# A GPS layer on one core: a histogram in the gather stage replaced by a search in the second norm, which is rewritten, and scalings moved between VectorE and ScalarE

## The reference, cut to what matters

```python
xn = layernorm(x)
x  = x + gcn(xn, src, dst) + linear_attention(xn)
x  = x + gat_experts(layernorm(x), src, dst)
# gcn:  h = relu(batchnorm(xn @ w1.T + b1)) @ w2.T + b2;  xw = h @ w_gcn.T
#       out[d] = sum over edges (s,d) and loops of xw[s] * dinv[s] * dinv[d], + b_gcn
# gat:  h = (x @ W_gat) as 4 heads x 4 experts; e = leaky_relu(a_src[src] + a_dst[dst])
#       softmax of e over the edges of each dst; agg = sum alpha * h[src]
#       layernorm, mean over heads -> scores; top 2 of 4 experts, softmax -> weights
#       out = sum over experts of weight * (gelu(x @ W1 + b1) @ W2 + b2)
```

## Time and profile before

| | before |
|---|---|
| median of 3 runs | 4779.59 us |
| lowest to highest | 4776.38 to 4796.87 us |
| profiled execution, its time | 4790.88 us |
| its span | 4789.0 us |
| PE busy | 3688.3 us, 77% |
| PEld busy | 2442.9 us, 51% |
| DVE busy | 2604.3 us, 54% |
| ACT busy | 880.5 us, 18% |
| POOL busy | 3085.5 us, 64% |

### The profile page before, as it was taken

The page is one execution under the profiler, slowest core; times in us unless marked ns, Lnnn a source line. Parts: engine busy times, 40 slices in busy tenths (PEclk is TensorE's granted clock), DMA queues, the critical chain, the costliest instruction groups (busy, mean ns, idle before and its releaser), DMA issues. The chain is left out here.

```text
span 4789.0 us, 44151 instructions
## 1 busy us (share of the span) xinstructions
PE 3688.3 (77%) x13162; PEld 2442.9 (51%) x13162; DVE 2604.3 (54%) x6218; ACT 880.5 (18%) x1738; POOL 3085.5 (64%) x3019
## 2 busy tenths in 40 slices
PE   3667888888798998787887564799999999700377
PEld 1355555455555555555555354466666666500255
DVE  5946776666666556666666364134334333312476
ACT  2653222222100000000000011222222223200232
POOL 2515777777776776777777500777777777777630
PEclk7989999999887998777677655899999999955689
DMA  6645444444454664333333765444444334322588
GB/s 178 188 98 152 129 130 132 130 130 130 125 154 132 182 177 131 89 91 89 92 91 89 71 193 137 132 114 113 138 115 113 117 106 138 97 63 63 114 209 196
DMA packets 262492, 606.63 MB, mean 127 GB/s; under 512 B 88254, under 2 KB 144369, under 8 KB 256893
## 3 DMA queue, kind: packets, MB, share of 16 engines
q0 software_dynamic: 124496, 304.94, 24.1%
q1 hardware_dynamic: 137772, 299.02, 22.2%
HBM read 447.85 MB, written 155.88 MB: 126 GB/s over the span
## 5 line engine op out<-in xcount | busy, mean ns | idle before, releaser
L1039 POOL DMA_INDIRECT g_rows<-table,gcn_srcT x1664 | 1758.2, 1057 | 568.0 <-issue 485.7
L1109 PE MATMUL g_ps<-g_rows,g_hot 128*125 128x256 f32 x3328 | 1064.3, 456 | 337.4 <-issue 229.6
L1902 POOL DMA_INDIRECT n_rows<-gtab,so_own x1122 | 1095.6, 977 | 341.9 <-issue 341.9
L1394 DVE TENSOR_TENSOR acc<-acc,g_ps 125x256 f32 x1664 | 696.4, 419 | 691.6 <-PE g_ps L1109 565.6
L1109 PEld LDWEIGHTS g_ps<-g_rows,g_hot 128*125 128x125 f32 x3328 | 685.8, 223 | 622.8 <-issue 410.0
L1842 PE MATMUL p_ph<-f_xfT,f_w 128*128 128x500 f32 x1344 | 576.7, 585 | 64.2 <-DMA f_xfT<-xfT_d 64.2
L1848 PE MATMUL p_py<-f_w,f_hh 128*125 128x256 f32 x2688 | 590.4, 379 | 0.0
L1848 PEld LDWEIGHTS p_py<-f_w,f_hh 128*125 128x125 f32 x2688 | 504.5, 188 | 101.1 <-issue 27.4
L2045 DVE TENSOR_TENSOR p_ob<-p_py,p_xb 125x512 f32<-125x512 f32 x168 | 115.6, 691 | 699.0 <-PE p_py L1848 698.6
L1842 PEld LDWEIGHTS p_ph<-f_xfT,f_w 128*128 128x128 f32 x1344 | 256.4, 191 | 348.6 <-issue 343.5
L2073 ACT ACTIVATE f_hh<-p_ph,f_b 128x500 f32<-128x500 f32 x336 | 221.4, 677 | 616.4 <-PE p_ph L1842 616.1
(11 more groups left out here) (338 smaller groups left out, 4329.8 us busy)
## 6 DMA issues: line engine op xcount, KB each, us to landing
o_d<-p_ob SPq DMA_DIRECT2D x21, 1920.0 KB
z_ob<-o_d SPq DMA_DIRECT2D x21, 1920.0 KB
g_rows<-table,gcn_srcT POOLq DMA_INDIRECT x1664, 3.0
n_rows<-gtab,so_own POOLq DMA_INDIRECT x1122
gout<-n_o SPq DMA_DIRECT2D x33, 408.0 KB, 2.5
xnT_d<-a_xnT SPq DMA_DIRECT2D x25, 500.0 KB
m_area<-xnT_d SPq DMA_DIRECT2D x25, 500.0 KB, 3.8
qT_d<-m_area SPq DMA_DIRECT2D x25, 500.0 KB, 3.1
```

Of the source, the lines that this page charges most:

```text
L1039: pool.indirect_dma_start(out=rows[:, g % RING, j], out_offset=None, in_=K.table, in_offset=bass.IndirectOffsetOnAxis(ap=K.gcn_srcT[:, 4 * ...
L1109: mm = pe.matmul(ps[q, p % 4, b], hot[:, g % 4, 2 * j + b], rows[:, g % RING, 2 * j + b], start=True, stop=True, skip_group_check=True)
L1394: dve.tensor_tensor(a, a, ps[q, p % 4, b], ALU.add).then_inc(add_s, 1)
L1902: pool.indirect_dma_start(out=rows[:, c % 3, j], out_offset=None, in_=K.gtab, in_offset=bass.IndirectOffsetOnAxis(ap=K.gat_src[:, c * W + ...
```

## The change

*First stage.* The fill of `gtab` and its buffer go. VectorE computes a third value per tile, `off` = -mean/root, and scales tiles 0 and 1; ScalarE scales tiles 2 and 3. SyncE and TensorE wait for both.

```diff
                     if k >= 3:
-                        sp.wait_ge(xn_s, (k - 2) * SUB)
+                        sp.wait_ge(xn_s, (k - 2) * (SUB // 2))
+                        sp.wait_ge(xna_s, (k - 2) * (SUB // 2))
                     rows_in_two(sp, xin[:, k % 3], A.x[k * BN:(k + 1) * BN].rearrange("(j p) f -> p j f", p=TN), x_in[k % 3])
...
 
-                sp.wait_ge(blank_s, 1)
-                sp.dma_start(K.gtab.rearrange("(t p) f -> p t f", p=TN)[:, :, TROW:TWIDE],
-                             blank[q].unsqueeze(1).to_broadcast([TN, NT, TWIDE - TROW])).then_inc(blank_s, 16)
                 for k in range(NB):
...
-                    pe.wait_ge(xn_s, (k + 1) * SUB)
+                    pe.wait_ge(xn_s, (k + 1) * (SUB // 2))
+                    pe.wait_ge(xna_s, (k + 1) * (SUB // 2))
                     if k:
...
+                def normalise(k):
+                    s = k % 2
+                    act.wait_ge(off_s, k + 1)
+                    if k >= 2:
+                        act.wait_ge(turned, (k - 1) * KC)
+                    for j in range(SUB // 2, SUB):
+                        act.activation(xn[q, s, j], xin[q, k % 3, j], ACT.Identity, bias=off[q, s, j:j + 1],
+                                       scale=rs[q, s, j, 0:1]).then_inc(xna_s, 1)
+
                 def inside(g):
                     act.wait_ge(got[g % DEEP], 64 * (g // DEEP + 1))
...
                     for ch in range(KC):
                         act.wait_ge(turned, k * KC + ch + 1)
                         act.copy(xnT[:, k % 2, ch], ptr[:, ch, 0:BN]).then_inc(xnT_s, 1)
+                    if k + 1 < NB:
+                        normalise(k + 1)
                     if k in (1, 2):
...
                     dve.wait_ge(root_s, k + 1)
                     dve.reciprocal(rs[q, s, :, 0], rs[q, s, :, 1]).then_inc(rec_s, 1)
                     dve.wait_ge(rec_s, k + 1)
+                    dve.scalar_tensor_tensor(off[q, s], mv[q, s, :, 0], -1.0, rs[q, s, :, 0], ALU.mult, ALU.mult
+                                             ).then_inc(off_s, 1)
                     if k >= 2:
                         dve.wait_ge(turned, (k - 1) * KC)
-                    for j in range(SUB):
+                    for j in range(SUB // 2):
                         dve.tensor_scalar(xn[q, s, j], xin[q, k % 3, j], mv[q, s, j, 0:1], rs[q, s, j, 0:1],
                                           ALU.subtract, ALU.mult).then_inc(xn_s, 1)
```

```diff
                         sp.dma_start(K.gcn_tiles[:], K.gcn_td.rearrange("(a s) -> a s", a=1)).then_inc(tile_s, 16)
-                    sp.wait_ge(acc_s, (k + 1) * SUB)
+                    sp.wait_ge(acc_s, (k + 1) * 2)
+                    sp.wait_ge(row_s, (k + 1) * 2)
                     rows_in_two(sp, K.table[k * BN:(k + 1) * BN].rearrange("(j p) f -> p j f", p=TN),
...
-                    for j in range(SUB):
+                    for j in (0, 2):
                         t = k * SUB + j
...
                         dve.wait_ge(px_s, 2 * k + a + 1)
                         if k >= 2:
-                            dve.wait_ge(acc_s, (k - 1) * SUB)
+                            dve.wait_ge(acc_s, (k - 1) * 2)
                         dve.tensor_tensor(tmp[q, k % 2, two], px[q, k % 2, two],
                                           K.b_both[q].unsqueeze(1).to_broadcast([TN, 2, D]), ALU.add).then_inc(tmp_s, 1)
+                    for a in range(2):
+                        j = 2 * a + 1
+                        t = k * SUB + j
+                        dve.wait_ge(tmp_s, 2 * k + a + 1)
+                        dve.tensor_scalar(K.acc[q, t], tmp[q, k % 2, j], K.dinv[q, t:t + 1], None, ALU.mult
+                                          ).then_inc(row_s, 1)
                     if k + 1 in at:
                         split_up(at.index(k + 1))
```

```diff
 HIST = MIX2 + NB * W2 + 10
 SLOTS = S_GCN // 2
+PIECE = GC // 3
+PIECES = LIST // PIECE
 
...
-                sp.dma_start(raw_d, A.edge_index[1].rearrange("(p c) -> p c", p=P)).then_inc(raw_s, 16)
+                sp.wait_ge(back, SHORT)
+                sp.dma_start(K.gat_dst.rearrange("(p i) h -> p (i h)", p=P), short).then_inc(kept_s, 16)
+                sp.wait_ge(kept_s, 16)
...
-                    if 0 <= p - HIST - W3 < half * W3:
-                        degrees(p - HIST - W3)
+                    if p == HIST + 2:
+                        pe.wait_ge(back, SPREAD)
+                        pe.matmul(pa[q, 0:PIECES], K.ones[:, q], spread.rearrange("p k i -> p (k i)"), start=True, stop=True
+                                  ).then_inc(head_s, 1)
...
-                pe.wait_ge(last_s, 1)
...
-                def degrees(i):
-                    r, at = divmod(i, W3)
-                    if at > 1:
-                        return
-                    cols = slice(r * HB, (r + 1) * HB)
-                    if r >= 2:
-                        dve.wait_ge(used, r - 1)
-                    if at == 0:
-                        dve.tensor_tensor(on[:, r % 2], number, node_h[:, cols].unsqueeze(1).to_broadcast([P, TN, HB]),
-                                          ALU.is_equal).then_inc(node_s, 1)
-                    else:
-                        wide = [P, HB, NT]
-                        dve.tensor_tensor(ot[:, r % 2], K.iota_h[:, 0:NT].unsqueeze(1).to_broadcast(wide),
-                                          tile_h[:, cols].unsqueeze(2).to_broadcast(wide), ALU.is_equal).then_inc(tile_s, 1)
...
+                def heads_below(t):
+                    if t == 0:
+                        dve.wait_ge(head_s, 1)
+                        dve.wait_ge(above_s, 2)
+                    if t >= 4:
+                        dve.wait_ge(met_s, t - 3)
+                    dve.tensor_scalar(met[q, t % 4], pa[q, 0:PIECES], above[q, t:t + 1], None, ALU.is_lt, ALU.add,
+                                      accum_out=before[q, t:t + 1]).then_inc(met_s, 1)
...
+                    then(dve.tensor_copy(sample, high.rearrange("p (i h) -> p i h", h=PIECE)[:, :, 0]))
+                    then(dve.tensor_copy(short, high))
+                    assert nb[0] == SHORT
+                    yield
                     then(dve.tensor_scalar(K.goes, low, float(SELF), None, ALU.is_ge))
+                    then(dve.tensor_tensor(spread, K.ident[:].unsqueeze(2).to_broadcast([P, P, 3]),
+                                           sample.unsqueeze(1).to_broadcast([P, P, 3]), ALU.mult))
...
                     yield
+                    for at, of in ((K.gat_head[:, 0:1], odd[:]), (K.gat_src, K.opens.bitcast(I32))):
+                        then(dve.tensor_scalar(of, at, 1.0 / TN, 0.5 / TN - 0.5, ALU.mult, ALU.add))
+                        then(dve.tensor_scalar(at, at, float(NT), None, ALU.mult))
+                        yield
+                        then(dve.scalar_tensor_tensor(at, of, float(1 - TN * NT), at, ALU.mult, ALU.add))
...
                         second(k, r)
-                    numbers(p - HIST + 3)
-                    if 0 <= p - HIST < half * W3:
-                        degrees(p - HIST)
...
-                dve.wait_ge(used, half)
-                dve.tensor_copy(by_tile[0:NT], pa[0:NT, q]).then_inc(last_s, 1)
-                dve.wait_ge(lastp, 1)
-                dve.tensor_copy(cnt2[q], pa[q, 0:NT]).then_inc(last_s, 1)
...
-                dve.tensor_tensor(K.gat_last[q], upto[q], ends[q], ALU.add).then_inc(last_s, 1)
+                dve.tensor_scalar(K.gat_last[q], before[q], -1.0, 0.0, ALU.add, ALU.max).then_inc(chosen, 1)
 
 
 def second_norm(nc, K, A):
```

More of the change, by code:

```diff
@@ L1777, in _ @@
[L1777 to L1784 removed]
+                        dve.wait_ge(st_s, k * SUB + j + 1)
```

366 lines of the change are left out of this document (193 added, 173 removed).

## The result

| | before | with the change |
|---|---|---|
| median, same chip, 4 runs each | 4786.39 us | 4614.65 us (4602.81 to 4626.94) |
| ratio of the two | | 0.9641, 95% interval 0.9605 to 0.9677 |
| profiled execution, its time | 4790.88 us | 4626.94 us |
| its span | 4789.0 us | 4625.2 us |
| PE / DVE / ACT / POOL busy | 3688.3 / 2604.3 / 880.5 / 3085.5 us | 3477.6 / 2466.7 / 960.9 / 3126.3 us |

The kernel is 3.6% faster, by 172 us. 4584 was forecast, and the range of 4545 to 4635 held the result. Both kernels ran four times, and the one before had its median 7 us above the 4779.59 from which the forecast was taken. The profiled execution of the change was the slowest of its four.

The account below looks back on a forecast made before the run. VectorE was taken to bound the first stage, GpSimd the gathers, no engine the norm. Terms -45 - 12 - 1 - 87 - 4 + 4 - 50 = -195 gave 4596 profiled, median 4584; forecast case 4555 to 4605, range 4545 to 4635.

Parts of the forecast that it names:

- rival A: Second norm stage slower than its bytes, 8.3 us per block, losing 31 us of the sum: 4615; chance 0.17.
- The fill: First stage: without the fill of gtab, block 3 of x loads early and VectorE is not held: -45 us.
- first norm: First stage: half the scalings move to ScalarE, -0.5 us per block over 24 blocks: -12 us.
- table: Table stage: VectorE scales two tiles that ScalarE scaled, and only the last block's rows get shorter: -1 us.
- Rival B: First stage: ScalarE sets the pace and the block stays at 7.3 us: 4596; chance 0.15.
- The histogram: Gather stage: without the histogram, 502 gathers go from 1.156 to 0.983 us each: -87 us.
- Rival C: Gather stage: PSUM comparisons or adds still hold GpSimd, -20 us instead of -87: 4651; chance 0.06.
- The last gathers: End of the gather stage: the chain of small steps closing the histogram behind the last gather falls away: -4 us.
- The list preparation: Gather stage: some eight more operations in the list preparation: +4 us, bounds 0 to +10.
- Second norm: Rewritten norm stage: blocks at 7.0 us set by DMA, -14, a shorter tail, -37, attention-vector fold, +1: -50 us.
- The tail: End of the second norm: table arithmetic and store become a copy, small store and last comparisons, 4 us: -37 us.
- Rival E: Expert stage: TensorE's granted clock comes back lower, making the kernel slower than before, 4853 at 0.80; chance 0.03.

Follow-up runs that it names:

- u_fill: The changed kernel with the fill of gtab's padding put back at its old place in SyncE's queue; median 4646.26 us, 0.9672 of the kernel before.
- u_split: The changed kernel with the first norm's scaling of all four tiles back on VectorE; median 4617.47 us, 0.9625 of the kernel before.
- h_sbuf: The changed kernel with 64 rounds of the histogram's two SBUF comparisons put back on VectorE, result unread; median 4719.82 us, 0.9825 of the kernel before.
- h_psum: The changed kernel with 256 further VectorE comparisons read from PSUM, result unread; median 4607.75 us, 0.9592 of the kernel before.
- p_spread: The changed kernel with the 128 padding entries naming 128 different table rows instead of row 0; median 4595.11 us, 0.9562 of the kernel before.
- n_late: The changed kernel with five piece buffers instead of three and second-norm search comparisons four blocks behind instead of two; median 4594.82 us, 0.9581 of the kernel before.
- n_nosearch: The changed kernel without the search's gathers and comparisons beside the second norm; median 4562.58 us, 0.9500 of the kernel before.
- repeat: The changed kernel run once more as it is; median 4607.29 us over 5 runs, 0.9613 of the kernel before.
- l_yield: The changed kernel with the renumbering's two big operations in two turns of the list preparation instead of one; median 4610.21 us, 0.9610 of the kernel before.

## Why the prediction was right, and where it was off

In the profiled execution the sum should have been -195 and was -164. On the chip of the last runs, against the median there, it is -190. The first median, 4614.65, equals rival A's 4615 by coincidence: A wanted norm blocks of 8.3 us. By its own terms:

- **The fill, -45; first norm, -12; table, -1.** Together -58, in the trace -57.5. By u_fill the first is 46, by u_split the second is 10. The new operation for `off` took 0.16 us, for 0.2 put down. ScalarE took its two scalings at 27.3/50 = 0.546 us each and not at 0.447, the price of the row at L835 worked out in the same way (a copy with a scale, without a bias), and still did not pace the block. Rival B is out at 6.73 us.
- **The histogram, -87.** Measured -92.5, by h_sbuf +99.6 when it is put back. The step from 1.156 to 0.983 was sized from the 60 gathers after the histogram; it came to 0.970. The mechanism was right, and the traces make it sharper: a gather is held when it begins inside an operation with two operands in SBUF. h_psum and the single gathers show why the new comparisons are free. What is left above 0.947 us, 13.7 us over the stretch, comes from the one-hot builds. Rival C is out.
- **The last gathers, -4.** Measured -6.7 up to the first c_x. I had called the landing of 12.4 us the padding's own cost, and p_spread shows it to be that: 15 us could be had.
- **The list preparation, +4.** Measured +8.7, within its bounds. I counted operations and did not look at what TensorE had to spare there, about a tenth; that this is why they cost twice the forecast is likely, not shown.
- **Second norm, -50.** Measured -37.7: mis-sized in two terms. The body was taken at 7.0 us per block; the profiled run has 7.19, the mean of nine is 7.07. The term was right for the wrong reason in part: I had the DMA full at 7.0, with 320 and 265 GB/s for its two queues, and n_late runs the same bytes in 6.73. Two of the terms beside it were off as well. TensorE's 6.1 was no floor, since n_nosearch has 5.72. And GpSimd's 5.0 was priced by a row gather; a gather of a piece takes 1.21 us (median) and 0.30 idle, so 6.0 per block. The tail, forecast at -37, is where the step failed. From last row copy to next stage it fell by 33.3, to 7.9 us and not to 4. And from last c_x to last row copy it rose from 16.7 to 21.2 us, and the prediction did not count how the pipeline runs empty. By its code the new stage works a block deeper, which fits; no run tests it. Rival A, 8.3 us per block, is out.
- **Gathers 5 to 844, 0.** Measured +21.8 in the one trace and 0 in the mean of twelve. No term was wrong here. But the forecast case's own range, 4555 to 4605, had no room for it, and the median of 4614.65 lies outside it. The stretch is TensorE's (996 of 1170 us busy), and its granted clock there is not the same twice.
- **Rival E** asked whether the experts' clock falls after 700 us of lighter TensorE work: 0.99 before, after and in repeat.

## What to carry to other kernels

Before work on VectorE is moved or counted beside GpSimd's gathers, compare single gathers with and without it in the trace: here a gather that began inside an operation with two operands in SBUF was held to its end, bf16 or f32. 193 us of such comparisons cost the gathers 100 us, and 156 us of comparisons out of PSUM cost them nothing. Cut two traces by the same work (here the number of the gather) before a difference is explained, and read a stretch that TensorE nearly fills from several executions; it alone moved by 40 us. A stage that is rewritten with a deeper pipeline may run out longer at its end (here 21.2 us instead of 16.7), so count the run-out as a term.

## What the runs showed of the hardware that was not expected

- Of 162 gathers in h_sbuf that begin inside an operation of VectorE with two operands in SBUF, 161 end 0.81 to 0.83 us after that operation; gathers that have begun before it, or run beside work with an operand in PSUM, take 0.95. The f32 one-hot builds alone do it too, 44 of 47 times in h_psum.
- 128 pieces of one row land in 11.7 us (median), 128 pieces of 128 rows in 2.8 us, with GpSimd's own time the same (0.946 and 0.947 us).
- A DMA share of 0.94 stood beside 283 GB/s in one kernel and beside 303 in another that stores one large transfer more per block; with the same pieces and other waits (n_late) it was 0.95 beside 300. By "DMA: Bandwidth & Descriptors" of the Trainium skill, section Specifications, HBM allows a core about 358 GB/s. Over a whole norm stage no run here came nearer than 303, so the trace neither shows that limit nor speaks against it.
- The granted clock over the same 840 gathers, with the same code in this stretch, was 0.91, 0.92 and 0.94 in three executions (the changed kernel, l_yield, repeat), with 1170, 1152 and 1143 us.
